# Second attention: moving VectorE's elu of the next group's queries ahead of the gate

## What is computed

```python
q = x @ Wq.T + bq ; u = x @ Wu.T + bu ; k = x @ Wk.T + bk ; v = x @ Wv.T + bv
u = silu(u) ; v = silu(v)
q = elu(q) ; k = elu(k)                       # 8 heads of 16
energy = einsum('bhnd,bhmd->bhnm', q, k) * tril(ones(256, 256))
out = einsum('bhnm,bhmd->bhnd', energy, v)    # no softmax
out = u * rms_norm(out, scale)
y = out @ Wo.T + bo
```

## Time and profile before

| | us |
|---|---|
| median of 3 runs | 913.0 (912.09 to 915.54) |
| profiled execution, its own time | 919.31 |
| its span, first to last instruction | 917.7 |
| PE busy | 837.2 (91%) |
| DVE busy | 702.9 (77%) |
| ACT busy | 571.4 (62%) |
| POOL busy | 621.1 (68%) |
| mean granted TensorE clock | 0.988 |

### The profile page before, as it was taken

The page is one execution under the profiler, slowest core; times in us unless marked ns, Lnnn a source line. Parts: engine busy times, 40 slices in busy tenths (PEclk is TensorE's granted clock), DMA queues, the critical chain, the costliest instruction groups (busy, mean ns, idle before and its releaser), DMA issues.

```text
span 917.7 us, 22375 instructions
## 1 busy us (share of the span) xinstructions
PE 837.2 (91%) x7975; PEld 748.0 (82%) x7975; DVE 702.9 (77%) x1809; ACT 571.4 (62%) x1183; POOL 621.1 (68%) x598
## 2 busy tenths in 40 slices
PE   3789999999899989998988989898999799999996
PEld 2678878989799989986666666666898699999996
DVE  6687877886476998897899998898653566668786
ACT  5766475444366667768886777563764466667562
POOL 4157676777304788775888788887777777766663
PEclk9999999999899999999999999999999999999999
DMA  9799997115648998972111111115685788799996
GB/s 263 214 381 358 362 353 255 50 50 167 241 130 275 312 303 258 281 229 68 40 42 40 39 38 44 40 44 190 217 270 198 227 275 262 260 303 341 361 363 183
DMA packets 130991, 191.06 MB, mean 208 GB/s; under 512 B 15809, under 2 KB 85953, under 8 KB 130753
## 3 DMA queue, kind: packets, MB, share of 16 engines
q1 hardware_dynamic: 96720, 141.21, 46.7%
q0 software_dynamic: 16640, 34.37, 11.6%
q10 hardware_dynamic: 17520, 14.06, 4.8%
HBM read 110.74 MB, written 80.97 MB: 209 GB/s over the span
## 4 chain that ended last, share of the span: by engine, by line
PE 54%; DVE 25%; POOL 6%; issue 6%; DMA 5%; ACT 4%; SPq 0%; DVEq 0%; ACTq 0%; POOLq 0%
PE pair L910 12%; PE pair L857 5%; PE pair L858 5%; PE pair L856 5%; PE pair L887 5%; PE pair L777 3%; POOL sent L2048 3%; PE pair L690 3%; DVE a_en L1606 2%; DVE X L1539 2%; PE pair L697 2%; DVE stats_t L1168 2%; PE pair L699 2%; PE pair L698 2%; DMA back<-ex_tile_out,address 2%
## 5 line engine op out<-in xcount | busy, mean ns | idle before, releaser
L2048 POOL DMA_INDIRECT sent<-a_rows,slot x224 | 220.6, 985 | 77.7 <-issue 58.0
L2150 POOL DMA_INDIRECT back<-ex_tile_out,address x136 | 151.8, 1116 | 60.0 <-issue 32.6
L2059 POOL DMA_INDIRECT ex_joined<-outs,slot x128 | 134.4, 1050 | 84.9 <-DMA outs<-ex_tile_out 48.0
L856 PE MATMUL pair<-ex_x_hi,ex_w_hi 128*128 128x256 f32 x497 | 147.6, 297 | 0.0
L857 PE MATMUL pair<-ex_x_lo,ex_w_hi 128*128 128x256 f32 x497 | 141.5, 285 | 0.0
L858 PE MATMUL pair<-ex_x_hi,ex_w_lo 128*128 128x256 f32 x497 | 141.5, 285 | 0.0
L910 PE MATMUL pair<-ex_stage,ex_hid 128*128 128x128 f32 x1136 | 132.5, 275 | 0.0
L910 PEld LDWEIGHTS pair<-ex_stage,ex_hid 128*128 128x128 f32 x1136 | 129.9, 192 | 0.0
L1746 ACT ACTIVATE ex_w_hi<-ex_stage 128x768 fp32r<-128x768 f32 (+1 forms) x72 | 67.5, 938 | 90.9 <-DMA ex_stage<-in_experts 90.9
L1872 ACT ACTIVATE ex_hid<-pair,ex_stage 128x256 f32<-128x256 f32 x284 | 107.2, 498 | 0.1
L1377 DVE TENSOR_TENSOR ex_w_lo<-ex_stage,ex_w_hi 128x768 fp32r<-128x768 f32 (+1 forms) x72 | 77.4, 1075 | 34.0 <-ACT ex_w_hi L1746 32.8
(11 more groups left out here) (253 smaller groups left out, 1999.9 us busy)
## 6 DMA issues: line engine op xcount, KB each, us to landing
ex_stage<-in_experts SPq DMA_DIRECT2D x72, 578.0 KB, 5.7
outs<-v_heads SPq DMA_DIRECT2D x8, 4352.0 KB, 36.7
ex_stage<-in_experts SPq DMA_DIRECT2D x72, 320.0 KB, 4.1
ex_tile_in<-sent SPq DMA_DIRECT2D x72, 128.0 KB
outs<-ex_tile_out SPq DMA_DIRECT2D x71, 128.0 KB
ex_joined<-back ACTq DMA_DIRECT2D x15, 512.0 KB, 8.1
ex_tile_in<-sent SPq DMA_DIRECT2D x54, 132.0 KB
X<-in_x SPq DMA_DIRECT2D x16, 256.0 KB, 5.3
```

What stands on the lines that cost most here:

```text
L856: pe.matmul(o[:, of_half], wh, x_hi[i % 2][:, of_half], start=True, stop=False)
L2048: pool.indirect_dma_start(out=sent[layer], out_offset=bass.IndirectOffsetOnAxis(ap=slot_i[layer][k][:, s, j:j + 1], axis=0), in_=rows[laye ...
L2059: pool.indirect_dma_start(out=joined[g % NJOIN][:, j, k, :], out_offset=None, in_=outs, in_offset=bass.IndirectOffsetOnAxis(ap=slot_i[0][k ...
L2150: pool.indirect_dma_start(out=back, out_offset=bass.IndirectOffsetOnAxis(ap=address[i % NSIDE][:, s // HALF, s % HALF:s % HALF + 1], axis= ...
```

## The change

The elu of the queries of group g + 1 moves from the start of VectorE's next step to the end of the present one, ahead of the gate. The first group keeps its elu at the start of step `LEAD`. As the elu now may run before the gate has waited for the second `gather`, it gets a wait of its own, for the first `gather` of group e, for the sake of the buffer of q1.

```diff
@@ -1630,7 +1630,7 @@
             for step in range(LEAD, STEPS1):
                 g, e, y, x = (step - LEAD - i for i in range(4))
                 new, old, last = 0 <= g < NG, 0 <= e < NG, 0 <= y < NG
-                if new:
+                if step == LEAD:
                     elu_plus_one(q1_exp, g, 0, e1[0], q1[g % 2], q1_max)
                 if 0 <= x < NG:
                     if with_root(x) is not None:
@@ -1666,6 +1666,10 @@
                     split_rows(1, 0, 4)
                 if last and with_root(y) is None:
                     inverse_rms(y)
+                if g + 1 < NG:
+                    if old:
+                        dve.wait_ge(av_done, 2 * e + 1)
+                    elu_plus_one(q1_exp, g + 1, 0, e1[0], q1[(g + 1) % 2], q1_max)
                 if old:
                     gated(e)
```

## The result

| us | before | after |
|---|---|---|
| median | 916.08 (20 runs, 912.09 to 921.5) | 919.22 (20 runs, 916.24 to 926.19) |
| profiled execution, its own time | 919.31 | 922.12 |
| its span | 917.7 | 920.5 |
| PE / DVE busy | 837.2 / 702.9 | 839.9 / 704.7 |
| ACT / POOL busy | 571.4 / 621.1 | 571.3 / 620.4 |

A forecast was written before the change was run, and what follows sets the result against it. VectorE was taken to set the pace in most steps of the second attention, TensorE in a few. 0.64 - 0.24 = +0.4 us on the median of 913.0 us gave 913.4 us, range 910.8 to 916.8 us.

The forecast's parts named there:

- The thirteen other swaps at 0: Swaps of elu and gate outside step 13's end: TensorE's earlier values only wait longer for residual and mask; worth 0.
- first rival: TensorE's waits for the elu pay in full, 5.9 us off the path: 907.1 us; chance 0.05.
- gone in six of seven places: Expected sign: TensorE's wait of the values for the elu vanishes in six of its seven places.
- The later gate on ScalarE at 0: ScalarE's squares and copy move 0.66 us later, covered by its idle time and TensorE's earlier values; worth 0.
- The second rival: The later gate holds ScalarE up at the squares, 0.66 us in each affected step; 918.3 us at seven; chance 0.07.
- The added waits at 0: The elu's added wait for the first gather, always met: 0 taken, 0.6 us for fourteen kept for the range.
- +0.64 us: End of step 13: VectorE waits 0.64 us for ScalarE's late exponential of the queries, with no cover behind it.
- The collision's price: VectorE product held by GpSimd's mask, from step 14 on: one more or fewer, up to 1.1 us either way, unsummed.
- The clock: Rival: a halved-clock stretch of TensorE vanishes or appears, 1.7 us either way: 911.7 or 915.1 us; chance 0.08.
- "-0.24 us" at the end of step 14: The elu fills VectorE's 0.28 us idle gap ahead of the gate; pair, residual and mask come 0.24 us earlier.
- the forecast's upper end: Top of the range, 916.8 us: up by a clock stretch, a collision and 0.6 us of added waits.
- The signed step, +0.4: Sum for the second attention, 0.64 - 0.24 = +0.4 us, giving 913.4 us from the median of 913.0 us.

The follow-up runs named there:

- exp_later: The change, with ScalarE's exponential of the routing at step 13's end moved behind step 14's four `minus_exp` instructions; ratio to the kernel before 1.0008 [0.9983, 1.0032].
- not13: The change without the swap at the end of step 13; 917.59 against 911.03 us for the kernel before, one run; ratios 0.9995 and 1.0001 in slower sets.
- delay64: The kernel before, no swap, with an extra VectorE product of about 0.64 us ahead of step 13's gate; ratio to the kernel before 1.0039 [1.0012, 1.0066].
- only13: The kernel before with only the swap at the end of step 13; ratio to the kernel before 1.0021 [1.0001, 1.0041].
- the set at 1018.5 us: First set of follow-up runs, named by the time of the kernel before in it, 1018.5 us in place of some 917, reason not known.

## Why the prediction was wrong

- **The thirteen other swaps at 0**: right. exp_later, with all fourteen, left the attention within 0.1 us and not13 within 0.4 us, each in one execution, and a wait for the residual follows as described. So the first rival (907.1 us) did not come. Its price was also too high by its own step: an elu 0.61 us earlier takes at most 0.61 from each of six waits, 3.7 us, not all 5.9. For the same reason "gone in six of seven places" was wrong: five waits remain.
- **The later gate on ScalarE at 0**: right. Squares waited 4.3 us where they waited 1.1, and nothing behind them was later. The second rival (918.3 us) lies near the measured time, by another mechanism.
- **The added waits at 0**: right as far as rows show. The elu at 499.56 stands directly behind its neighbour; exp_later, which keeps all fourteen, is within 0.1 us over the attention.
- **The step that failed is "+0.64 us" at the end of step 13.** The wait came in its size. The error was to hand 0.64 us down the queue as a plain sum: "Behind it stand the residual, the second choice of the routing and the mask that ended at 587.06". The second choice is five products and reductions on SBUF, and GpSimd's mask started 0.86 us behind the end of the last of them. That distance had to be checked against the shift, and the recorded times alone would not have been enough: 0.86 less 0.64 leaves 0.22 us. What was missing too is that the hold reaches ahead of the mask's recorded start. The trace of before had it: the addition at 477.82 started 0.62 us ahead of its mask and took 1.88 us, and the product of the earlier trace rows (it lies in step 7, not 6) started 0.44 us ahead. Shifted by 0.64 us, L1207 would have started at 586.26, 0.51 us ahead of the mask at 586.77, inside that reach; an estimate from these rows is that it ends 0.15 us behind the mask, about 1.5 us late beyond the shift. The prediction placed such meetings "from step 14 on", as chance, outside the sum. The runs showed 3.25 us in place of 0.64: 0.61 for the wait, 1.61 for the hold, 1.0 for the clock.
- **The collision's price**, "up to 1.1 us either way", was the time of the mask alone; it measured 1.61 us, since the hold begins ahead of the mask's recorded start. The addition at 477.82 had already lost 1.54 us that way (1.88 against 0.34 us).
- **The clock** was a rival, something that happens instead of the forecast. It came in addition. The same 2.2 us left TensorE idle just behind the fall, and the long halved stretch stands only in the two traces where it was (the change, delay64); that the idle time is the cause is a reading of these rows. The size was within the 1.7 us given. The reading behind it was not right: in the stage before the change the clock fell not once but twice, at 588.1 and at 639.3 us of the span, and again at 649.6, 3 us behind the last gate's end.
- **"-0.24 us" at the end of step 14**: the pair did gain it (3.0 against 3.25 us late), but it was not worth it. L1228 is held in both kernels until GpSimd's mask ends, and that swallowed it.
- **The base.** Three runs gave 913.0 us, twenty gave 916.1. From that base the forecast's upper end would have been 919.9, and the median of 919.22 inside. The signed step, +0.4, would still have been wrong.

## What to carry to other kernels

A swap that is neutral by the sum of its parts can shift everything behind it by a few tenths. Lay the shifted instructions against the other engine's timeline, one by one, down to the next point where the engines meet anyway, and do it first wherever VectorE runs products of two SBUF operands near a GpSimd instruction on SBUF. Leave a margin ahead of that instruction's recorded start: here products that started up to 0.65 us ahead of it were held. Look for such holds in the trace before the change, by the instructions whose time is several times that of the same line elsewhere. Before a swap puts a wait into an engine's stream, look for the one place where its input is late: here one of fourteen carried the loss, and in the trace with ScalarE's unrelated exponential moved behind what others wait for it was gone.

## What was not expected of the hardware

The hold on VectorE begins before the `affine_select` is recorded. Products that started 0.65 us (L1206, the change and only13), 0.46 us (L1207, delay64) and 0.17 us (L1207, delay64 in the set at 1018.5 us) ahead of it, while GpSimd's record shows the indirect send, all ended 0.15 or 0.16 us behind the select's end. One that started 0.78 us ahead (L1206, delay64) was free. As an estimate from these rows, the hold begins between 0.49 us ahead of the recorded start, where that free product ended, and 0.36 us, where L1206 of the change would have ended after its usual 0.29 us.

The products in only13 of the set at 1018.5 us were free as well: 0.50 us ahead, before ScalarE's copy had ended, and 0.18 us ahead, 0.04 us behind the copy's end. The rows fit a GpSimd that claims the memory port once it has reached the select and its operand is there; they fit as well a select that begins earlier than its recorded start. Neither is shown by itself. The Trainium skill, page "SBUF — State Buffer", section "SBUF: two separate sides", has the exclusion for a whole instruction, and the rows agree.

Two kinds of instruction were not held. In the kernel before a reduction with one SBUF input (L1190, 546.44, 0.28 us) ended 0.02 us ahead of a mask without loss, and VectorE's own mask of energies, with one operand in PSUM (L1606, 585.84), ran across the start of GpSimd's at 586.77 in its usual 1.22 us.

The halved clock fell at 588.1 us of the span in the kernel before, in the change and in only13, although the attention of only13 began 2.6 us earlier, and at 588.8 in delay64. It lasted 3.4 us where TensorE was busy from there on (before, only13) and 6.8 us where TensorE was idle for a part of the time just behind the fall (the change, delay64).
